# Cross attention: probabilities times values as one plain fp32 matmul per key tile instead of three fp32r matmuls

## The reference, cut to what matters

```python
q = (latents @ Wq).reshape(b, q_len, N_KV_HEADS, N_GROUPS, HEAD_DIM)
k = (hidden_states @ Wk).reshape(b, kv_len, N_KV_HEADS, HEAD_DIM)
v = (hidden_states @ Wv).reshape(b, kv_len, N_KV_HEADS, HEAD_DIM)
...
scores = jnp.einsum('bqhgd,bkhd->bhgqk', q, k) * scale
attn = jax.nn.softmax(scores.astype(jnp.float32), axis=-1).astype(q.dtype)
out = jnp.einsum('bhgqk,bkhd->bqhgd', attn, v)
out = out.reshape(b, q_len, N_HEADS * HEAD_DIM)
return out @ Wo
```

## Time and profile before

| | us |
|---|---|
| median of 2 runs | 2183.43 |
| the 2 runs | 2183.39, 2183.47 |
| span of the profiled execution | 2183.8 |
| TensorE busy with matmuls | 2113.8 (97% of the span) |
| TensorE busy with weight loads | 1939.3 (89%) |
| VectorE busy | 1264.0 (58%) |
| ScalarE busy | 1062.2 (49%) |
| GpSimd busy | 224.7 (10%) |

### The profile page before, as it was taken

One profiled execution on the slowest core, in us unless ns is written; L12 is line 12 of the kernel. 1 busy time (PEld: TensorE's weight loads), 2 busy tenths in 40 slices (PEclk: granted clock), 3 DMA queues, 4 the chain that ended last, 5 costly groups with the idle time before them and its releaser, 6 DMA issues. The chain is left out here.

```text
span 2183.8 us, 38297 instructions
## 1 busy us (share of the span) xinstructions
PE 2113.8 (97%) x14054; PEld 1939.3 (89%) x14054; DVE 1264.0 (58%) x2580; ACT 1062.2 (49%) x1596; POOL 224.7 (10%) x105
## 2 busy tenths in 40 slices
PE   8999999899999999999999999998789999999998
PEld 6888888799998999989999999997669999999876
DVE  5211111666766676767667676766664666666555
ACT  4111111556566665666566665655324455445442
POOL 0000001300022000130000310001310000000110
PEclk9999999999999999999999999999999999999999
DMA  6322221200011000120001200002634554445462
GB/s 231 109 103 96 77 97 50 81 25 13 24 57 64 17 22 24 44 78 13 25 12 45 86 14 26 13 15 95 252 120 172 189 193 178 173 178 191 141 229 79
DMA packets 57383, 199.26 MB, mean 91 GB/s; under 512 B 4592, under 2 KB 22000, under 8 KB 51760
## 3 DMA queue, kind: packets, MB, share of 16 engines
q1 hardware_dynamic: 57264, 197.71, 25.4%
HBM read 170.43 MB, written 27.26 MB: 91 GB/s over the span
## 5 line engine op out<-in xcount | busy, mean ns | idle before, releaser
L749 DVE TENSOR_TENSOR xa_pT_lo<-xa_t_ps,xa_pT_hi 128x512 fp32r<-128x512 f32 x544 | 373.0, 690 | 333.5 <-ACT xa_pT_hi L626 333.5
L626 ACT ACTIVATE xa_pT_hi<-xa_t_ps 128x512 fp32r<-128x512 f32 x544 | 321.8, 597 | 413.5 <-PE xa_t_ps L822 402.6
L105 PE MATMUL xa_o_ps<-xa_pT_hi,xa_v_hi 128*128 128x256 f32 x1088 | 310.0, 285 | 1.8 <-DVE xa_pT_lo L749 1.7
L107 PE MATMUL xa_o_ps<-xa_pT_hi,xa_v_lo 128*128 128x256 f32 x1088 | 308.2, 283 | 0.0
L106 PE MATMUL xa_o_ps<-xa_pT_lo,xa_v_hi 128*128 128x256 f32 x1088 | 307.8, 283 | 0.0
L822 PE MATMUL xa_t_ps<-ident,xa_rows 128*128 128x128 f32 x1632 | 294.4, 273 | 0.5 <-DVE xa_pT_lo L749 0.5
L724 DVE TENSOR_SCALAR_CACHE_REDUCE xa_rows<-xa_s_ps 128x512 f32<-128x512 f32 (+1 forms) x432 | 274.9, 653 | 0.6 <-PE xa_s_ps L107 0.6
L105 PE MATMUL xa_s_ps<-split,xa_qT_hi 128*128 128x512 f32 (+1 forms) x576 | 251.3, 436 | 2.2 <-POOL split L682 1.3
L620 ACT ACTIVATE xa_rows<-xa_rows,xa_neg_max 128x1088 f32<-128x1088 f32 x192 | 229.7, 1196 | 0.0
L105 PEld LDWEIGHTS xa_o_ps<-xa_pT_hi,xa_v_hi 128*128 128x128 f32 x1088 | 207.3, 191 | 16.4 <-DVE xa_pT_lo L749 3.1
L107 PE MATMUL xa_s_ps<-split,xa_qT_lo 128*128 128x512 f32 (+1 forms) x576 | 221.0, 384 | 0.0
(11 more groups left out here) (288 smaller groups left out, 4791.5 us busy)
## 6 DMA issues: line engine op xcount, KB each, us to landing
pair_raw<-in_w_qk SPq DMA_DIRECT2D x15, 2048.0 KB, 8.4
pair_raw<-in_w_gv SPq DMA_DIRECT2D x15, 2048.0 KB, 8.2
full<-in_wo SPq DMA_DIRECT2D x16, 1024.0 KB, 5.2
pair_raw<-in_w_out SPq DMA_DIRECT2D x16, 1024.0 KB, 5.1
xa_w_raw<-in_wq SPq DMA_DIRECT2D x31, 512.0 KB, 3.7
full<-in_ctxT SPq DMA_DIRECT2D x7, 2048.0 KB, 8.2
stage<-v_scratch SPq DMA_DIRECT2D x16, 544.0 KB, 4.1
kT_scratch<-kv_k_out SPq DMA_DIRECT2D x8, 1024.0 KB, 4.1
```

The source lines that it names most:

```text
L105: pe.matmul(out, w_hi, m_hi, start=first, stop=False)
L107: return pe.matmul(out, w_lo, m_hi, start=False, stop=last)
L626: act.activation(pT_hi[j % NPT][:, :, :], t_ps[:, (par * PAIRS + j) % 2, :, :], ACT.Copy).then_inc(pT_hi_ready, 1)
L749: dve.tensor_tensor(pT_lo[j % NPT][:, :, :], t_ps[:, (par * PAIRS + j) % 2, :, :], f32(pT_hi[j % NPT][:, :, :]), ALU.subtract).then_inc(pT ...
```

## The change

V is kept as one fp32 tile `v`, the turned probabilities as `pT` (fp32), and each of the 34 products of a head is one plain fp32 matmul. The copies of ACT stay, and they write fp32 instead of fp32r. DVE's subtractions of `dve_turned` are gone, as are POOL's subtractions for V. For a V piece POOL now only waits for the copy and raises `piece_lo`. TensorE waits for ACT's `pT_ready` where it waited for DVE's `pT_lo_ready`.

```diff
--- before.py
+++ after.py
@@ -449,8 +449,7 @@
 
     with ExitStack() as ctx:
         a = Alloc(nc, ctx, "xa_")
-        v_hi = a.sb("v_hi", [P, KV], F32R)
-        v_lo = a.sb("v_lo", [P, KV], F32R)
+        v = a.sb("v", [P, KV])
         kT_hi, kT_lo = shared.r
         rows = [[shared.f if (i, t) == (0, 0) else a.sb(f"rows{i}{t}", [P, KV]) for t in range(QT)] for i in range(2)]
         stage = [shared.stage[:, i * PIECE:(i + 1) * PIECE] for i in range(2)]
@@ -459,8 +458,7 @@
         w_lo = a.sb("w_lo", [P, KT, D], F32R)
         qT_hi = a.sb("qT_hi", [P, TOK], F32R)
         qT_lo = a.sb("qT_lo", [P, TOK], F32R)
-        pT_hi = [a.sb(f"pT_hi{i}", [P, 2, TOK], F32R) for i in range(NPT)]
-        pT_lo = [a.sb(f"pT_lo{i}", [P, 2, TOK], F32R) for i in range(NPT)]
+        pT = [a.sb(f"pT{i}", [P, 2, TOK]) for i in range(NPT)]
         maxima = a.sb("maxima", [P, 2, QT, UPR])
         neg_max = a.sb("neg_max", [P, 2, QT])
         sums = a.sb("sums", [P, 2, QT, PIECES])
@@ -492,8 +490,7 @@
         max_ready = a.sem("max_ready")
         exp_done = a.sem("exp_done")
         turned = a.sem("turned")
-        pT_hi_ready = a.sem("pT_hi_ready")
-        pT_lo_ready = a.sem("pT_lo_ready")
+        pT_ready = a.sem("pT_ready")
         pv_done = a.sem("pv_done")
         sum_ready = a.sem("sum_ready")
         ones_set = a.sem("ones_set")
@@ -602,7 +599,7 @@
                 act.wait_ge(pv_done, NPT + PAIRS * (GROUP * g - 1) + -(-end // (2 * P)))
             if i >= 2 * PIECES - 2:
                 act.wait_ge(pv_done, NPT + PAIRS * GROUP * g)
-            to = (kT_hi if i < PIECES else v_hi)[:, end - PIECE:end]
+            to = (kT_hi if i < PIECES else v)[:, end - PIECE:end]
             act.activation(to, stage[i % 2][:, :], ACT.Copy).then_inc(piece_hi, 1)
 
         def act_weight(act, n):
@@ -623,8 +620,8 @@
         def act_turned(act, n, par, j):
             act.wait_ge(turned, PAIRS * n + j + 1)
             act.wait_ge(pv_done, pt_free(n, j))
-            act.activation(pT_hi[j % NPT][:, :, :], t_ps[:, (par * PAIRS + j) % 2, :, :],
-                           ACT.Copy).then_inc(pT_hi_ready, 1)
+            act.activation(pT[j % NPT][:, :, :], t_ps[:, (par * PAIRS + j) % 2, :, :],
+                           ACT.Copy).then_inc(pT_ready, 1)
 
         def act_slot(act, g, n, u, last):
             par = u % 2
@@ -659,6 +656,7 @@
             act.sem_inc(spread_copied, 1)
             act.sem_inc(w_hi_ready, 1)
             act.sem_inc(piece_hi, FIRST)
+            act.sem_inc(pT_ready, 2)
             act_query(act, 0)
             for i in range(FIRST, PIECES):
                 act_piece(act, 0, i, first=True)
@@ -677,9 +675,12 @@
 
         def pool_piece(pool, g, i):
             pool.wait_ge(piece_hi, 2 * PIECES * g + i + 1)
+            if i >= PIECES:
+                pool.wait_ge(piece_lo, 2 + 2 * PIECES * g + i)
+                pool.sem_inc(piece_lo, 1)
+                return
             at = slice(i % PIECES * PIECE, (i % PIECES + 1) * PIECE)
-            hi, lo = (kT_hi, kT_lo) if i < PIECES else (v_hi, v_lo)
-            pool.tensor_tensor(lo[:, at], stage[i % 2][:, :], f32(hi[:, at]), ALU.subtract).then_inc(piece_lo, 1)
+            pool.tensor_tensor(kT_lo[:, at], stage[i % 2][:, :], f32(kT_hi[:, at]), ALU.subtract).then_inc(piece_lo, 1)
 
         def pool_weight(pool, n):
             pool.wait_ge(w_hi_ready, n + 1)
@@ -744,11 +745,6 @@
                 dve.scalar_tensor_tensor(out=diag_lo[:, at], in0=ident[:, :], scalar=inverse[:, qt:qt + 1],
                                          in1=f32(diag_hi[:, at]), op0=ALU.mult, op1=ALU.subtract).then_inc(diag_ready, 1)
 
-        def dve_turned(dve, n, par, j):
-            dve.wait_ge(pT_hi_ready, PAIRS * n + j + 1)
-            dve.tensor_tensor(pT_lo[j % NPT][:, :, :], t_ps[:, (par * PAIRS + j) % 2, :, :],
-                              f32(pT_hi[j % NPT][:, :, :]), ALU.subtract).then_inc(pT_lo_ready, 1)
-
         def dve_output(dve, n, par):
 
             dve.wait_ge(spread_copied, n + 2)
@@ -763,8 +759,6 @@
             for j in range(PAIRS):
                 if j == PAIRS - 1:
                     dve_output(dve, n, par)
-                if has_next or j + LAG < PAIRS:
-                    dve_turned(dve, *ahead(n, par, j))
                 if has_next:
                     for k in UNITS_OF_STEP[j]:
                         dve_scores(dve, n + 1, 1 - par, k)
@@ -776,15 +770,12 @@
         @block.vector
         def _(dve):
             dve.sem_inc(s_drained, NS)
-            dve.sem_inc(pT_lo_ready, 2)
             dve.sem_inc(o_ready, 1)
             dve_query(dve, 0)
             dve.wait_ge(shared.k_stored, 16 * (NCHUNK + 2))
             for k in range(NU):
                 dve_scores(dve, 0, 0, k)
             dve_query(dve, 1)
-            for j in range(LAG):
-                dve_turned(dve, 0, 0, j)
             slots(dve, dve_slot)
 
 
@@ -815,7 +806,7 @@
 
             done = piece_of(2 * P * (j + 1)) + 1
             pe.wait_ge(exp_done, QT * PIECES * n + PIECES * (QT - 1) + done)
-            pe.wait_ge(pT_lo_ready, PAIRS * n + j + 1)
+            pe.wait_ge(pT_ready, PAIRS * n + j + 1)
             for t in range(2):
                 at = slice((2 * j + t) * P, (2 * j + t + 1) * P)
                 for qt in range(QT):
@@ -829,11 +820,11 @@
                 pe.wait_ge(piece_lo, 2 + 2 * PIECES * g + PIECES + piece_of(2 * P * (j + 1)) + 1)
             if j == 0:
                 pe.wait_ge(o_ready, n + 1)
-            pe.wait_ge(pT_lo_ready, 2 + PAIRS * n + j + 1)
+            pe.wait_ge(pT_ready, 2 + PAIRS * n + j + 1)
             for t in range(2):
                 at = slice((2 * j + t) * P, (2 * j + t + 1) * P)
-                last = three_pass(pe, o_ps[:, par, :], v_hi[:, at], v_lo[:, at], pT_hi[j % NPT][:, t, :],
-                                  pT_lo[j % NPT][:, t, :], j == 0 and t == 0, j == PAIRS - 1 and t == 1)
+                last = pe.matmul(o_ps[:, par, :], v[:, at], pT[j % NPT][:, t, :], start=j == 0 and t == 0,
+                                 stop=j == PAIRS - 1 and t == 1)
             last.then_inc(pv_done, 1)
 
         def pe_slot(pe, g, n, u, last):
```

## The result

| | us |
|---|---|
| before, median of 2 runs (2183.39 to 2183.47) | 2183.43 |
| changed, median of 2 runs (2241.55 to 2244.83) | 2243.19 |
| ratio, 95% interval | 1.0271 [1.0242, 1.0301] |
| predicted, with its range | 2264 (2246 to 2312) |
| span of the profiled execution, before and changed | 2183.8, 2243.0 |

The direction was right. A second sample of four runs of the changed kernel gave 2246.25 us, 59 us over the 2187.26 of the kernel before on the same chip (ratio 1.027 [1.0253, 1.0287]).

A forecast was written before the change was run, and what follows sets the result against it. TensorE's streaming was taken as the bound: 2183.8 us, +92.5 for the plain fp32 products, -8.9 for diagonal waits, -1.7 for the half clock, -1.7 for waits before products with V, gave 2264 us (range 2246 to 2312).

The forecast's parts named there:

- Rival C: Products with V: two records at the fp32r pace, 118 ns each, 237 per product, 2042 us; chance 0.08.
- D: Products with V: weight loads not hidden behind the other record's stream, 330 ns per record, 2503 us; chance 0.04.
- B: Products with V: dearer passes, 460 to 473 ns per product, 2286 to 2300 us; chance 0.24.
- F: Products with V: a price near today's, 345 to 395 ns, total within 2%; chance 0.03.
- E: Cross attention: half clock granted in places with fewer, longer matmuls, some 2270 to 2400 us; chance 0.03.
- A: The forecast itself: products with V at 427 to 450 ns each, 2264 us; chance 0.58.
- The term of the product: 1088 products with V on TensorE, 440 ns each instead of 355: +92.5 us, between +78 and +128.
- the upper case: Products with V: a product as four fp32r matmuls at 118 ns, 473 ns, giving +128 us.
- The term of the waits: TensorE's waits: -8.9 us before line 853, -1.7 for the half clock, -1.7 before products with V.
- The low end: Whole kernel: 427 ns per product, all 12 us of waits and part of the 6.2 gone, 2246 us.
- the stretch in the last head: After the last head's wait: 3.4 us at a granted clock of 0.50 should not come, -1.7 us.
- The waits at the turns: Before line 822 at outer loop turns: 2 us waits, supposedly the loop's jump, stay; 0, gain bounded by 6.2 us.

The follow-up runs named there:

- the halves of 128: Changed kernel with each plain fp32 product cut into two of 128 columns: 2262.34 us against 2246.25 for the changed kernel on the same chip.
- the run with the earlier diagonals: Kernel before with DVE's inverse sums and diagonals one step earlier, two in the last head: 2174.15 us against 2187.26, ratio 0.9938.

## Why the prediction was right and where it was wrong

**The main mechanism was right.** TensorE bounds the stage, a plain fp32 matmul is two records, each streams about two cycles a column, and that is more than three fp32r matmuls. A steady step with two score units was to become 2.72 us and is 2.69 (904.15 to 906.84). Rival C (two fast records) and D (loads not hidden) are excluded by the 215 ns; B (460 to 473 ns) and F (345 to 395) as well, and E by a granted clock of 1.00 from 409 to 1580 us. The price lies in A's band of 427 to 450.

**The term of the product was mis-sized: 92.5 us forecast, 80 measured** (1088 x 74 ns). I took 440 ns from the distance of the transposes, 110 ns for 128 columns, and scaled it with the columns, as if all of it were their stream. But 256 columns take 215 ns and 512 take 429, and the halves of 128 fell back to 111. The 2 to 4 ns over the stream's 107, be they the pace of the weight load or a fixed part of a record, do not grow with the columns. The evidence stood in the same rows: line 1043 had the same 110 ns with one column to stream, so 110 could not tell a stream of 107 ns from none at all. The lengths in the earlier trace rows did show two cycles a column, and 4 x 107 = 427 was the better price. The Trainium skill's rule of four passes ("FP8 and Floating Point Precision", section TensorE Precision Notes) agrees with the time of 430 ns when a pass is priced at one column per cycle; priced at this trace's fp32r pace, as I did for the upper case, it does not.

**The term of the waits was mis-sized: 12.3 us forecast, 21 measured, and this put the time outside the range.** The low end allowed 78 us of price, close to the 80 measured, and at most 16 us back. Had the product been priced right, 12.3 us for the waits would have given 2251.5 us: inside the range, but still 8 us too long. Each wait that I named went as I said. Of the half clock I had only the stretch in the last head. The kernel before had two more in the stage (columns as in the earlier trace rows, the granted clock third from the end):

```profile
408.60:412.00 3.40, 3.40 (x13) 2.81 (x12) 1.78 (x5) 1.59 (x2) 1.03 (x1) 0.50 0.65 240
691.90:695.30 3.40, 3.40 (x14) 3.01 (x13) 1.91 (x5) 1.59 (x2) 1.39 (x1) 0.50 0.35 133
```

Not in my list, or too small in it, were:
- the half clock behind the wait at the first turn of the outer loop (passes of 256 columns stand 0.21 us apart there, 0.12 at the full clock); it costs 1.6 us and does not occur in the changed kernel's trace;
- stalls before a product in the three heads where K pieces arrive, 0.60 to 0.76 us each by the starts, 2.8 us with the slower starts right behind them, where the view of waits lists 1.5;
- the waits before line 853 at the V pieces, 1.4 us each by the starts where the view lists 1.2;
- the two turns, kept at nothing, which are 1.0 us shorter together;
- in the last two heads 8.8 us, where I had 5.3 + 1.7: some 1.3 us more are three short waits for DVE's subtractions (at 1490.5, 1493.4 and 1497.2 us);
- 2.0 us at the entry of the stage, a wait 0.7 us shorter and the half clock at 408.6, and 0.5 after the stage.

I had summed the waits that a view lists. The distances between the starts of one line in successive heads (34.55 us undisturbed, up to 38.4 around a turn) would have shown at once that 13 us are lost before the last two heads, where the view lists 3.6 for the diagonals, 3.7 for the turns and 1.5 for the products, and that would have given a lower low end. How much of it would go could not be read from them: in the kernel before the half clock stands behind the first turn and not behind the second.

**DVE and POOL.** For the last head I had named both halves of the cause, for the V pieces POOL's instruction alone. It stood up; the runs add that DVE's lateness is the other half there too: with POOL's subtractions alone nothing waits. The Trainium skill has the rule ("SBUF — State Buffer", section SBUF: two separate sides): DVE and GpSimd share a port pair that one of them holds for a whole instruction, if the DVE instruction runs in a two-port mode, or has two SBUF inputs while the GpSimd instruction reads SBUF. These traces agree: the diagonals, with SBUF operands only, took 2.9 to 3.2 us a pair beside POOL, and the subtraction of line 749, which reads one operand from PSUM, kept its length during POOL's 4.72 us above and everywhere in the kernel before:

```profile
L749 DVE TENSOR_TENSOR xa_pT_lo<-xa_t_ps,xa_pT_hi x544: 674/691/694, 407.6 to 1517.4; 128x512 fp32r<-128x512 f32 x182
```

**The waits at the turns.** I kept them and supposed the loop's jump. Writing the loop out removed the two at the turns. The third, at the entry, was not the jump.

What stays open: why an fp32r matmul takes 118 ns for 256 columns and 230 for 512, 8 to 11% over one cycle a column, when the plain fp32 records have 1% on top of two. No run here varied what could cause it.

## What to carry to other kernels

A plain fp32 matmul costs four cycles a column on TensorE, in two records with a load each: 430 ns at 256 columns and 858 at 512, for 355 and 696 of a three-matmul fp32r split. In a kernel that TensorE bounds, the work it saves on other engines gives back only what TensorE waited for, here 21 us against a price of 80. Whether it pays where those engines are the bound was not tried. When a price is read from the distance of short matmuls, ask first whether the weight load sets that distance: a row with fewer columns and the same distance says it does. When the gain of removed work is read from waits, take it from the distance of the same line in successive rounds, which also holds the short stalls and the half clocks that a list of waits leaves out. And before giving up exact arithmetic or engine work to be rid of a wait, look at where in the engine's own order the late instruction stands: here one call, moved by one step (two in the last head), gave three quarters of what dropping 560 subtractions gave (13 us of 17).

## What the runs showed of the hardware that I had not expected

- Plain fp32 records stand 215 ns apart at 256 columns and 429 at 512, within 1% of two cycles a column at 2.4 GHz, while fp32r matmuls in the same step need 118 and 230 ns for one.
- Two kinds of small DVE operations on 128x128 (285 and 348 ns) took up to 2379 and 2629 ns beside POOL's subtractions (the earlier trace rows has the second). Where two POOL instructions followed each other without a gap, 2.3 us each, one DVE operation ended behind each of them: 1502.69 to 1505.07 and 1504.99 to 1507.43 us in the kernel before.
- A turn of the outer hardware loop leaves TensorE idle for 1.1 to 2.0 us, and the profile puts it down to a semaphore that the next instruction names, or to issue; turns of the inner loop, two heads long, cost nothing that shows.
- Line 1043's eight records of one column, 110 ns apart at the full clock, stand 211 ns apart (2049.85 to 2051.54 us) in the run with the earlier diagonals, where the granted clock was 0.51: the pace of the loads follows TensorE's clock.
